# Joining the short stages of a four-layer graph network kernel: layernorm with its transpose and the result gathers, table stores with what makes the table, statistics with the product

## What is computed

```python
def _layernorm(x, axis=-1, eps=1e-05):
    m = jnp.mean(x, axis=axis, keepdims=True)
    v = jnp.var(x, axis=axis, keepdims=True)
    return (x - m) / jnp.sqrt(v + eps)
...
def _gin_conv(x, src, dst, n, W1, b1, gamma, beta, W2, b2):
    agg = jax.ops.segment_sum(x[src], dst, num_segments=n)
    h = x + agg
    h = jax.nn.relu(_batchnorm(h @ W1 + b1, gamma, beta))
    return jax.nn.relu(h @ W2 + b2)
```

## Time and profile before

| | |
|---|---|
| median of 3 runs | 7234.84 us (7220.34 to 7235.94) |
| the profiled execution | 7225.76 us, span 7224.1 us |
| busy: TensorE matmul / VectorE / ScalarE / GpSimd | 5038.9 / 3353.9 / 1675.0 / 3374.7 us |
| mean granted TensorE clock | 0.819 of full speed |
| HBM read / written | 472.47 MB / 121.17 MB |

### The profile page before, as it was taken

One profiled execution on the slowest core, in us unless ns is written; L12 is line 12 of the kernel. 1 busy time (PEld: TensorE's weight loads), 2 busy tenths in 40 slices (PEclk: granted clock), 3 DMA queues, 4 the chain that ended last, 5 costly groups with the idle time before them and its releaser, 6 DMA issues. The chain is left out here.

```text
span 7224.1 us, 73624 instructions
## 1 busy us (share of the span) xinstructions
PE 5038.9 (70%) x20207; PEld 3266.0 (45%) x20208; DVE 3353.9 (46%) x7945; ACT 1675.0 (23%) x4060; POOL 3374.7 (47%) x3515
## 2 busy tenths in 40 slices
PE   5946766676638588867774499389998459576545
PEld 1214444444415233345553388378885234343334
DVE  5953334333515466666667011456665442343412
ACT  2930002000212367731112122133333111000111
POOL 4026772666250266657770555266660120666322
PEclk6968888777869689977777699699999779788877
DMA  4013332333110000023330577233340134333245
GB/s 178 2 54 91 91 91 58 89 91 91 32 48 1 22 2 2 2 70 90 91 90 9 160 220 213 69 101 103 106 99 16 52 96 146 90 91 91 51 144 170
DMA packets 405755, 597.99 MB, mean 83 GB/s; under 512 B 131359, under 2 KB 305759, under 8 KB 405279
## 3 DMA queue, kind: packets, MB, share of 16 engines
q0 software_dynamic: 144992, 337.62, 17.4%
q1 hardware_dynamic: 257200, 252.99, 11.3%
q10 hardware_dynamic: 3216, 3.28, 0.1%
HBM read 472.47 MB, written 121.17 MB: 82 GB/s over the span
## 5 line engine op out<-in xcount | busy, mean ns | idle before, releaser
L711 PE MATMUL ps<-zerow,zerob 128*128 128x440 bf16 x2640 | 812.3, 394 | 655.1 <-issue 399.4
L699 POOL DMA_INDIRECT wide<-table,src x880 | 882.0, 1002 | 792.7 <-ACTq L95 404.4
L741 DVE TENSOR_TENSOR sums<-sums,ps 128x256 f32 x1320 | 555.3, 421 | 1237.3 <-PE ps L714 490.4
L714 PE MATMUL ps<-wide 128*128 128x256 f32 x2640 | 906.8, 428 | 20.1 <-DMA wide<-table,src 7.9
L711 PEld LDWEIGHTS ps<-zerow,zerob 128*128 128x128 bf16 x2640 | 245.3, 104 | 999.7 <-issue 569.8
L714 PEld LDWEIGHTS ps<-wide 128*128 128x128 f32 x2640 | 568.8, 219 | 195.0 <-issue 60.6
L699 POOL DMA_INDIRECT wide<-table_rel,rel x440 | 437.8, 995 | 417.0 <-ACTq L95 218.5
L1642 POOL DMA_INDIRECT wide<-table_gat,src x440 | 472.5, 1074 | 218.4 <-issue 121.9
L2255 POOL DMA_INDIRECT work<-table,work x440 | 442.6, 1006 | 262.5 <-PE ps L2292 129.4
L1530 POOL DMA_INDIRECT work<-table_max,src x440 | 438.4, 996 | 198.9 <-issue 128.5
L1549 PE MATMUL ps<-wide,work 128*128 128x512 f32 x880 | 491.0, 642 | 0.0
(11 more groups left out here) (446 smaller groups left out, 9246.1 us busy)
## 6 DMA issues: line engine op xcount, KB each, us to landing
wide<-in_L_ffn_W SPq DMA_DIRECT2D x64, 1024.0 KB
wide<-in_L_ffn_expert_w SPq DMA_DIRECT2D x90, 256.0 KB
table_rel<-wide SPq DMA_DIRECT2D x20, 1024.0 KB
work<-rows_in SPq DMA_DIRECT2D x62, 256.0 KB
rows_out<-work SPq DMA_DIRECT2D x62, 256.0 KB
work<-rec SPq DMA_DIRECT2D x110, 136.0 KB
rec<-work SPq DMA_DIRECT2D x27, 544.0 KB, 16.4
wide<-table,src POOLq DMA_INDIRECT x880
```

Source lines behind the costliest of these rows:

```text
L699: nc.gpsimd.indirect_dma_start(rows[:, w % RT, :], None, table, bass.IndirectOffsetOnAxis(ap=index[:, w:w + 1], axis=0)).then_inc(gathered ...
L711: nc.tensor.matmul(m.PS[:, w % (2 * Q), 0:WT], m.zerob[:, 0:P], m.zerow[:, 0:WT], start=True, stop=True)
L714: nc.tensor.matmul(m.PS[:, w % (2 * Q), 0:D], S[:, w % RT, :], rows[:, w % RT, :], start=True, stop=True).then_inc(summed, 1)
L741: v.tensor_tensor(at, at, m.PS[:, s, 0:D], ALU.add).then_inc(added, 1)
```

## The change

- `layernorm` now also makes the transpose, and works in five groups of five tiles: statistics of group g + 1 on VectorE, then normalisation of group g (three tiles on VectorE, two on ScalarE); TensorE transposes straight from `dst`, ScalarE takes 23 transposed tiles out of PSUM, VectorE the last two. With `picks` it holds the gathers and additions of `fetch_rows` as well (then normalisation of g comes ahead of the statistics of g + 1). The `turn` behind it is gone, the one in `gates` too.
- `store_table` is gone. `normalise_nodes` and `gin_output` store five pieces of five tiles from SyncE as they are made, and GpSimd copies each tile to `m.AGG`. In the edge network the store and the clearing of `m.AGG` (now on GpSimd) run in the next `linear_nodes`.
- `linear_features` takes the statistics of `batch_stats` on VectorE block by block. Two small loads more stand ahead of its first matmul.
- `linear_nodes` and `linear_features` use eight PSUM banks; the ring copy of `linear_nodes` is gone.
- `gates` holds the second layernorm: statistics on VectorE ahead of the logits, 14 tiles normalised by ScalarE, 11 by GpSimd.
- The output is stored in five pieces in the last `fetch_rows`.

```diff
+def layernorm(nc, m, src, dst, dstT, picks=0, shared=True, ready=None):
...
+            moments(0)
+            for g in range(GROUPS):
+                if picks:
+                    normal(g)
+                if g + 1 < GROUPS:
+                    moments(g + 1)
+                if not picks:
+                    normal(g)
+            for n in range(NT - LAST_BY_DVE, NT):
+                t = order[n]
+                dve.wait_ge(turned, n + 1)
+                v.tensor_copy(dstT[:, :, t * P:(t + 1) * P], m.PS[:, n % 8, 0:D].rearrange("p (k n) -> p k n", k=KD))
 
         @block.scalar
...
+            for g in range(GROUPS):
+                mine = slice(g * U, g * U + U)
+                act.wait_ge(vared, g + 1)
+                nc.scalar.activation(rstd[:, mine], rstd[:, mine], ACT.Sqrt).then_inc(rooted, 1)
+                if g:
+                    evict((g - 1) * U)
+                    evict((g - 1) * U + 1)
+                act.wait_ge(shifted, g + 1)
+                for t in range(g * U, g * U + BY_ACT):
+                    nc.scalar.activation(dst[:, t, :], src[:, t, :], ACT.Identity, bias=shift[:, t:t + 1],
+                                         scale=rstd[:, t:t + 1]).then_inc(normed_a, 1)
+                if g:
+                    for n in range((g - 1) * U + 2, g * U):
+                        evict(n)
+            for n in range(NT - U, NT - LAST_BY_DVE):
+                evict(n)
...
-def store_table(nc, m, src, table, sums=None):
...
+def linear_nodes(nc, m, srcT, weight, bias, width, finish, stores=None):
...
+            if stores is not None:
+                sp.dma_start(m.table.rearrange("(t p) d -> p t d", p=P), stores[:]).then_inc(stored, 16)
+                sp.wait_ge(stored, 16)
+
+        @block.gpsimd
+        def _(pool):
+            if stores is not None:
+                nc.gpsimd.memset(m.AGG[:], 0.0)
...
+def normalise_nodes(nc, m, zT, dst, table):
...
+        @block.sync
+        def _(sp):
+            for t in range(0, NT, U):
+                sp.wait_ge(taken, t + U)
+                sp.dma_start(rows[:, t:t + U, :], dst[:, t:t + U, :]).then_inc(stored, 16)
+            sp.wait_ge(stored, 16 * (NT // U))
+
+        @block.gpsimd
+        def _(pool):
+            for t in range(NT):
+                pool.wait_ge(taken, t + 1)
+                nc.gpsimd.tensor_copy(m.AGG[:, t, 0:D], dst[:, t, :])
...
+def linear_features(nc, m, srcT, weight, bias, dstT, gamma, beta):
...
+            sp.dma_start(gb[:, 0, :], gamma).then_inc(loaded, 16)
+            sp.dma_start(gb[:, 1, :], beta).then_inc(loaded, 16)
...
+            for i, (lo, hi) in enumerate(cuts):
+                for j in range(KD):
+                    dve.wait_ge(taken, i * KD + j + 1)
+                    ins = v.bn_stats(stats[:, j, 6 * i:6 * i + 6], dstT[:, j, lo:hi])
...
+            if again:
+                act.wait_ge(vared, 1)
+                nc.scalar.activation(rstd, rstd, ACT.Sqrt).then_inc(rooted, 1)
+                act.wait_ge(shifted, 1)
+                for t in range(BY_ACT):
+                    nc.scalar.activation(m.XN[:, t, :], m.XN[:, t, :], ACT.Identity, bias=shift[:, t:t + 1],
+                                         scale=rstd[:, t:t + 1])
...
+                pool.wait_ge(shifted, 1)
+                for t in range(BY_ACT, NT):
+                    nc.gpsimd.tensor_scalar(m.XN[:, t, :], m.XN[:, t, :], rstd[:, t:t + 1], shift[:, t:t + 1],
+                                            ALU.mult, ALU.add)
```

More of the change, by code:

```diff
@@ new lines, in moments @@
+            def moments(g):
+                tiles = range(g * U, g * U + U)
+                for t in tiles:
+                    if picks:
+                        results(t)
+                        dve.wait_ge(whole, t + 1)
+                    ins = v.bn_stats(stats[:, t, :], src[:, t, :])
+                c.step(ins)
+                for t in tiles:
+                    ins = v.bn_aggr(mv[:, t, :], stats[:, t, :])
+                c.step(ins)
+                mine = slice(g * U, g * U + U)
+                v.tensor_scalar(rstd[:, mine], mv[:, mine, 1], EPS, None, ALU.add).then_inc(vared, 1)
@@ new lines, in _ @@
+            for n in range(NT - U, NT - LAST_BY_DVE):
+                evict(n)
+        @block.tensor
+        def _(pe):
+            for n, t in enumerate(order):
+                g, s = divmod(t, U)
+                if s < BY_ACT:
+                    pe.wait_ge(normed_a, g * BY_ACT + s + 1)
+                else:
+                    pe.wait_ge(normed_v, g * (U - BY_ACT) + s - BY_ACT + 1)
+                if n >= 8:
+                    pe.wait_ge(evicted, n - 7)
+                for k in range(KD):
+                    mm = nc.tensor.transpose(m.PS[:, n % 8, k * P:(k + 1) * P], dst[:, t, k * P:(k + 1) * P],
+                                             m.ident[:])
+                mm.then_inc(turned, 1)
@@ new lines, in _ @@
+            for i in range(CHUNKS):
+                for j in range(KD):
+                    n = i * KD + j
+                    if n >= BANKS:
+                        pe.wait_ge(taken, n - BANKS + 1)
+                    for k in range(KD):
+                        mm = nc.tensor.matmul(m.PS[:, n % BANKS, 0:CH], w[:, k, j * P:(j + 1) * P],
+                                              srcT[:, k, i * CH:(i + 1) * CH], start=(k == 0), stop=(k == KD - 1))
+                    mm.then_inc(made, 1)
@@ L961, in _ @@
             sp.dma_start(b, bias.unsqueeze(0).to_broadcast([P, D])).then_inc(loaded, 16)
+            if table is not None:
+                rows = table.rearrange("(t p) d -> p t d", p=P)
+                for t in range(0, NT, U):
+                    sp.wait_ge(taken, t + U)
+                    sp.dma_start(rows[:, t:t + U, :], m.XN[:, t:t + U, :]).then_inc(stored, 16)
+                sp.wait_ge(stored, 16 * (NT // U))
+        @block.gpsimd
+        def _(pool):
+            if table is not None:
+                for t in range(NT):
+                    pool.wait_ge(taken, t + 1)
+                    nc.gpsimd.tensor_copy(m.AGG[:, t, 0:D], m.XN[:, t, :])
@@ L1025, in slice_attention @@
     HW = H * QG
-    layernorm(nc, m, m.X, m.XN)
-    turn(nc, m, m.XN, m.XT)
+    layernorm(nc, m, m.X, m.XN, m.XT)
     weights = view(m.BB, 0, NT, HW)
@@ L2131, in _ @@
             c.step(v.memset(prob, -1.0))
+            if again:
+                for t in range(NT):
+                    ins = v.bn_stats(stats[:, t, :], m.XN[:, t, :])
+                c.step(ins)
+                for t in range(NT):
+                    ins = v.bn_aggr(mv[:, t, :], stats[:, t, :])
+                c.step(ins)
+                v.tensor_scalar(rstd, mv[:, :, 1], EPS, None, ALU.add).then_inc(vared, 1)
+                dve.wait_ge(rooted, 1)
+                c.step(v.reciprocal(rstd, rstd))
+                v.scalar_tensor_tensor(shift, mv[:, :, 0], -1.0, rstd, ALU.mult, ALU.mult).then_inc(shifted, 1)
             dve.wait_ge(turned, NT)
@@ L2185, in edge_update @@
     linear_nodes(nc, m, m.XT, w1[D:2 * D, :], None, D, keep(by_dst))
-    store_table(nc, m, by_dst, m.table, sums=0.0)
-    linear_nodes(nc, m, m.XT, w1[0:D, :], a["L2_gnn_b1"], D, keep(by_src))
+    linear_nodes(nc, m, m.XT, w1[0:D, :], a["L2_gnn_b1"], D, keep(by_src), stores=by_dst)
     CW = D + 1
```

370 lines of the change are left out of this document (176 added, 194 removed).

## The result

The changed kernel takes **7100.94 us** (median of four runs, 7090.2 to 7104.71) beside 7231.72 us for the kernel before (7220.34 to 7235.94): a ratio of 0.9831, 95% interval 0.9817 to 0.9845, 1.7% faster. The profiled execution took 7100.32 us, so the profiles give a saving of 125.4 us where the sum had 141.7.

The account below looks back on a forecast made before the run. No stage overlaps the next, so time was taken as the sum of stage lengths. Savings summed to 141.7 us: 7225.8 becomes 7084 us profiled, 7093 as median, 7088 us said; range 7062 to 7125 us.

Parts of the forecast that it names:

- Layernorm with turn: Six layernorms joined with their transposes: 23.1 us each, from 172.0 us together, saving 33.4 us.
- the wait of 1 us: End of each joined layernorm: VectorE, ready at 18.1 us, waits 1 us for ScalarE's last root at 19.1 us.
- Gathers in the layernorm: Two layernorms holding gathers, GpSimd setting the two-row pace: 72.5 for 96.9 us and 41.7 for 65.2, saving 24.4 and 23.5.
- Rival (a): Joined stages: VectorE's work holds up 75 gathers by 0.87 us each, losing 65 us, 7153 us in all; chance 0.07.
- Rivals (b) to (d): (b) TensorE stays at 1.2 GHz, 7133 us, 0.05; (c) no overlap, 7205 us, 0.02; (d) slower aggregation gathers, 7299, 0.02.
- Stores in parts: Normalisation, GIN output and program end: only the last five-tile piece stays outside, ending 4.1 us behind the last tile; saves 25.8 us.
- store beside the product: Edge network: table store and clearing of sums run beside a 29.5 us product, removing the 11.9 us in front of it.
- Statistics in the product: Two products with statistics taken block by block: 31.0 for 37.9 us each, saving 13.8 us.
- Router: Second layernorm moved into the router: 31.3 for 43.8 us, including 1.5 us for a colder TensorE; saves 12.5 us.
- TensorE's clock: Products behind joined layernorms begin at 1.2 GHz, losing 1.1 to 1.5 us in three stages besides the router: -3.6 us.
- rival (b): Products behind the joined layernorms: TensorE stays at 1.2 GHz, costing 45 us more, 7133 us in all; chance 0.05.

Follow-up runs that it names:

- the first comparison: The changed kernel against the kernel before, ahead of the follow-up experiments: 7100.94 us beside 7231.72 us, ratio 0.9831.
- the other slow trace: The kernel before, unchanged, traced again in a later comparison, in which it took 7158.38 us.
- three edits: Changed kernel with statistics first (81.3 and 49.2 us), GpSimd held back four tiles (73.0 and 42.6 us), or VectorE staggered (74.6 and 42.2 us) in layernorms with gathers.

## Why the prediction was right, and where not

- **Layernorm with turn** (33.4 us, found 37.7): right, with the wait of 1 us in its place. It was sized 0.7 us long per stage; and taking the wait away gains 0.15 us or less, since ScalarE's evictions take its place.
- **Gathers in the layernorm** (24.4 and 23.5 us, found 4.1 and 12.4): this is the step that failed in the first comparison. "The gathers still set the pace until the last addition" was right at the fast level, to 0.6 us in both stages, and wrong at the slow one. There the joining of the two-row gathers is worth nothing: the fetch apart (68.9 us at that level) and a joined layernorm behind it (22.7) make 91.6 us, an estimate from two traces, for 92.8 joined; with one row it is 58.8 for 52.8. I priced VectorE's work beside the gathers from the earlier trace rows, rows of a stage in which VectorE only waits for arrivals. The earlier trace rows had held the warning: 91.1 us of GpSimd's idle time in the aggregations ends with a releaser called "remote", and I read that as slack of those stages, not as a state that every stage with VectorE and GpSimd beside each other takes part in.
- **Rival (a)**, gathers held up by VectorE, had the place right and the direction wrong: GpSimd lost nothing (50 gathers busy 47.96 us), VectorE did, 31 us of the 65 that it was priced at. The row that priced it, the 1.82 us of the earlier trace rows, is nothing of the level. That gather was issued 0.23 us into a VectorE instruction with two inputs in SBUF, 1024 elements a partition long:

```profile
800.91 1.22 DVE L126 TENSOR_TENSOR wide<-iota,lo 128x1024 f32<-128x1024 f32 x1
```

and it ended 0.83 us behind that instruction's end. So did, within 0.06 us, all 73 gathers of the changed kernel's three aggregations that took over 1.2 us at the slow level, and all 24 at the fast one. The joined stages' additions have two inputs in SBUF too but are over in 0.5 us, so a gather issued beside them, which takes 0.96 us anyway, is held for 0.1 us at most (the longest took 1.06 us). Rivals (b) to (d) didn't come: the first aggregations took 660.2 and 657.8 us.
- **Stores in parts** (25.8, found 26.7) and **store beside the product** (11.9, found 11.8): right. The first adds up to 26.0 from its own lengths, not 25.8. VectorE's copy of the last tile of the normalisation stage ends at 451.23 us, the piece is issued at 451.26, and the barrier is done at 455.68, 4.4 us later (4.1). GpSimd's copy of 128x256 takes 0.40 us (0.5).
- **Statistics in the product** (13.8, found 12.3): the last block's statistics and the aggregates take 0.50 and 0.60 us (0.4 and 0.55 in the forecast); both products took 0.4 to 1.1 us longer than forecast.
- **Router** (12.5, found 15.8): the chain is the forecast one. Half of the 3.3 us is the colder TensorE (1.5 us) that didn't come: up to the last logits the granted clock was 0.90, as before. The rest is the sum: its terms, from 17.0 us on, add up to 28.0 and not to the 29.8 us written, and 28.08 was measured. GpSimd's 11 tiles took 0.54 us each and ended before ScalarE. The table load shows its 1.28 us and no idle time on either side:

```profile
3868.50 6.99 ACT L2210 ACTIVATE normed<-normed,work 128x256 f32<-128x256 f32 x14 [0.60 <-DVE work L2246]
3875.49 1.28 ACT L2216 ACT_TABLE_LOAD   x1
3876.78 0.24 ACT L2216 ACTIVATE work<-work 128x50 f32<-128x50 f32 x1
```

- **TensorE's clock** (-3.6 us): the product behind the joined layernorm ran at 0.89 and cost nothing (27.49 us for 27.68). The block L3_ffn paid instead: the product ahead of its router took 17.7 us for 16.6, at 0.81 for 0.90, and its router 25.28 us for 21.58, because the load of its bias let TensorE start 3.7 us into the stage and not 1.8 us, after 5.0 us of idle time, and at 1.2 GHz (granted clock 0.50 for the first 2.8 us, 1.00 before); it did so at both levels. Why the load came later is open.

Against the kernel before at the fast level 152 us were saved, against the slow one 131. The forecast sum of 141.7 lies between. No trace of the kernel before exists at the fast level, so the 152 us can't be split into terms. That the median was met to 13 us is in part luck: the misses were 31 us one way and some 15 the other, 7 in the smaller terms and 8 in the rest, of which 7.0 in a stage that the change doesn't touch (slice attention 250.8 to 243.8 us; the same stage of the kernel before took 218.2 us in the other slow trace).

The sum itself gives a median of 7093 us; for the 7088 that I said there is no reason in the working. The range has two slips as well: the lower end adds up to 7064 and not 7062, and rival (b), named as giving the upper end of 7125, stands at 7133.

## What to carry to other kernels

Putting vector work beside GpSimd's gathers is worth the whole time that it fills where VectorE keeps its pace, and a third of it here where it doesn't (16.5 us of 47.9); a row from a stage in which VectorE only follows arrivals says nothing on that. Before an experiment is read, let the unchanged kernel run beside it: here three edits looked like three cures, and the disease wasn't there to be cured. A wait that a chain of waits shows isn't worth its length unless what queues behind it on the next engine gets shorter too.

## Not expected of the hardware

One program took 6594 to 6599 and 7158 to 7232 us on the same kind of chip, the two levels in two comparisons running on a chip with the same number (6599, then 7158 us), with engines' busy times much alike. At the slow level some of VectorE's instructions, also such as wait for nothing, start 0.7 or 1.4 us apart in the joined stages with gathers, from some 19 to 42 us into the stage until some 4 to 7 us after the last issue. ScalarE starts late there too where it waits for a value (0.5 to 5.4 us after it is made); in between its copies kept their pitch (0.25 us) and GpSimd's gathers theirs (1.26).

Of the gather issues that start while VectorE runs a 1.22 us instruction with two inputs in SBUF, those that take long all end some 0.83 us behind that instruction's end, 1.98 us after their start at the longest instead of 0.96, at either level.
